# Feed-forward over the even rows of tiles first, in one program with the long convolution

## The reference, cut to what matters

```python
x = x + tanh(g_xattn[0]) * xattn(layernorm(x), ctx, mask, mask, Wq, bq, Wk, bk, Wv, bv)
x = x + tanh(g_ffn[0])   * ffn(layernorm(x), w_gate, w_up, w_down)      # quantised rows, sigmoid(gate) * up
x = x + tanh(g_xattn[1]) * longconv(layernorm(x), k, fside, ctx, ctx, 8)
x = x + tanh(g_ffn[1])   * fp8_layer(layernorm(x), w_fc, w_proj)

def longconv(v, k, bias, x1, x2, num_heads):           # B, D, L = v.shape; H = D // num_heads
    kv = vr[:, :, :, None, :] * x2r[:, :, None, :, :]  # products within a group of 8 channels
    y = causal_convolution(kv, k)                      # along L, one filter per group (by FFT in the reference)
    y = y + kv * bias
    return einsum('bhijl,bhil->bhjl', y, x1r)

def ffn(x, w_gate, w_up, w_down):
    h = sigmoid(bitlinear(x, w_gate)) * bitlinear(x, w_up)
    return bitlinear(h, w_down)                        # bitlinear: each row is scaled by its maximum and rounded
```

## Time and profile before

| | us |
|---|---|
| median of 3 runs | 1246.86 (1246.72 to 1247.12) |
| the profiled execution | 1245.74 |
| its span | 1243.9 |
| TensorE busy | 1075.5 (86%) |
| VectorE busy | 997.0 (80%) |
| ScalarE busy | 695.9 (56%) |
| GpSimd busy | 514.3 (41%) |

### The profile page before, as it was taken

One profiled execution on the slowest core, in us unless ns is written; L12 is line 12 of the kernel. 1 busy time (PEld: TensorE's weight loads), 2 busy tenths in 40 slices (PEclk: granted clock), 3 DMA queues, 4 the chain that ended last, 5 costly groups with the idle time before them and its releaser, 6 DMA issues. The chain is left out here.

```text
span 1243.9 us, 14018 instructions
## 1 busy us (share of the span) xinstructions
PE 1075.5 (86%) x4802; PEld 421.4 (34%) x4802; DVE 997.0 (80%) x1521; ACT 695.9 (56%) x835; POOL 514.3 (41%) x403
## 2 busy tenths in 40 slices
PE   4889689999999999778999967999999996279586
PEld 2444222222222222134444433444444443134232
DVE  4368679999999996298999955888788878677897
ACT  2777488888888888746666641110000000786996
POOL 2665323553543543611011017878887881000111
PEclk9999899999999999999999988999999997599889
DMA  9899733644644642051111110112212120000011
GB/s 325 268 380 385 241 114 104 194 128 136 192 125 135 197 123 92 28 195 51 35 52 35 52 38 29 57 52 68 68 51 68 52 67 1 0 1 1 18 51 68
DMA packets 73703, 132.89 MB, mean 107 GB/s; under 512 B 18336, under 2 KB 37152, under 8 KB 73120
## 3 DMA queue, kind: packets, MB, share of 16 engines
q1 hardware_dynamic: 73632, 132.00, 32.5%
HBM read 107.58 MB, written 22.02 MB: 104 GB/s over the span
## 5 line engine op out<-in xcount | busy, mean ns | idle before, releaser
L897 DVE TENSOR_REDUCE mneg<-ps_m 128x1 f32<-128x512 f32 x512 | 326.4, 685 | 40.0 <-PE ps_m L809 36.3
L1470 PE MATMUL ps_y<-kv,toeplitz_sb 128*128 128x512 f32 x640 | 279.1, 595 | 8.8 <-POOL kv L1382 8.8
L749 ACT ACTIVATE probs<-ps_s 128x1024 f32<-128x1024 f32 x256 | 250.7, 1022 | 37.9 <-PE ps_s L842 37.8
L1470 PEld LDWEIGHTS ps_y<-kv,toeplitz_sb 128*128 128x128 f32 x640 | 120.9, 191 | 154.8 <-issue 154.8
L842 PE MATMUL ps_s<-qk_stack 128*128 128x512 bf16 x512 | 139.6, 387 | 29.2 <-ACT probs L749 28.2
L852 PE MATMUL ps_o<-probs,v_all 128*17 128x512 f32 x1024 | 135.8, 603 | 0.0
L1382 POOL TENSOR_TENSOR kv<-vT,ctxT_sb 128x2048 f32<-128x2048 f32 x32 | 118.7, 3711 | 39.2 <-PE ps_y L1470 32.1
L1088 PE MATMUL ps_g<-w,xT_f 128*128 128x512 bf16 x512 | 119.6, 382 | 11.5 <-DVE h_f L1254 7.9
L809 PE MATMUL ps_m<-qk_stack 64*128 64x512 bf16 x512 | 112.1, 392 | 15.2 <-DVE mneg L897 8.1
L1435 ACT ACTIVATE w_anchor<-w_f 128x512 f32<-128x512 f32 x32 | 20.1, 628 | 180.6 <-DMA w_f<-in_w 180.6
L1536 DVE TENSOR_TENSOR z<-ps_y,ctxT_sb 128x1024 f32<-128x1024 f32 x64 | 77.9, 1218 | 46.8 <-PE ps_y L1470 46.8
(11 more groups left out here) (163 smaller groups left out, 1613.7 us busy)
## 6 DMA issues: line engine op xcount, KB each, us to landing
qk_stack<-qk_parts SPq DMA_DIRECT2D x192, 128.0 KB, 2.9
w_sweep<-in_w SPq DMA_DIRECT2D x8, 1536.0 KB, 11.8
qk_parts<-qk_part SPq DMA_DIRECT2D x16, 768.0 KB, 9.0
w_sweep<-in_w SPq DMA_DIRECT2D x16, 768.0 KB, 5.5
w_sweep<-in_w SPq DMA_DIRECT2D x16, 512.0 KB, 3.6
toeplitz_sb<-in_toeplitz SPq DMA_DIRECT2D x32, 256.0 KB, 2.6
w_f<-in_w SPq DMA_DIRECT2D x32, 256.0 KB, 2.9
v_rows<-vp SPq DMA_DIRECT2D x8, 544.0 KB, 10.0
```

Of the source, the lines that this page charges most:

```text
L749: nc.scalar.activation(pr[:, k % 2, 2 * slot:2 * slot + 2, :], S[:, 2 * slot:2 * slot + 2, :], ACT.Exp).then_inc(exp_done, 1)
L897: nc.vector.tensor_reduce(mneg[:, h, tc, hd:hd + 1], M[:, bank_, :], AX.X, ALU.max, negate=True).then_inc(max_red, 1)
L1470: mm = nc.tensor.matmul(Y[:, q % 3, l2, :], T[:, g % 2, (lt - m) * P:(lt - m + 1) * P], kv[:, g % 2, m, :], start=(m == 0), stop=(m == lt))
```

## The change

The feed-forward takes the tiles in the order 0, 2, ..., 14, 1, 3, ..., 15 (`ORDER`). `ln_vector` is cut in two: `ln_variance` issues the seven small operations up to the variance, `ln_inverse` waits for ScalarE's square root and takes the reciprocal. There are six rounds of mean and deviation instead of five: the round before the convolution is split into the even tiles (round 3, in the feed-forward's tiles 9 and 10) and the odd ones (round 4, in the convolution's groups 0 and 1). ScalarE normalises the even tiles ahead, two in each of the tiles 12 to 15, into the part of vT that the odd tiles fill later. The eight turn-ins of even tiles and their copies go between the last operations of the feed-forward; the eight of the odd tiles go beside groups 2 to 9 instead of 0 to 7.

The two stages share one block, so the engines no longer meet between them. The buffers of the convolution lie at fixed places over buffers of the feed-forward that are out of use by then, with waits for that (`xq_ready`, `hq_ready`, `h_ready`, `d_taken`). GpSimd runs the all-reduce and the first products before the last update of the feed-forward, which stands behind the gains of group 0.

The diff, cut to its core; the body of `phase_longconv` that is the same but for its indentation is left out:

```diff
+LN_COLUMNS = (range(ROWT), range(ROWT - 2), range(ROWT - 2, ROWT), range(0, ROWT, CT), range(1, ROWT, CT), range(ROWT))
+ORDER = (*range(0, ROWT, CT), *range(1, ROWT, CT))
...
-def ln_vector(core, dve, r):
+def ln_variance(core, dve, r):
...
+def ln_inverse(core, dve, r):
...
@@ tensor of phase_bitlinear
             if last:
+                pe.wait_ge(h_ready, NCH * ROWT - 1)
+                for i in range(2):
+                    turn_in(pe, i)
                 down(t - 1, 1 - par, False)
+                for i in range(2, ROWT // 2):
+                    turn_in(pe, i)
                 turn_h(t, par, False)
                 down(t, par, False)
@@ scalar of phase_bitlinear
                     copy_h(t - 1, 1 - par)
+                if c == 3 and t == ROWT // 2 + 1:
+                    ln_scalar(core, act, 3)
+                if c in (1, 3) and t >= ROWT - 4:
+                    normalise(act, 2 * (t - ROWT + 4) + c // 2)
             if last:
+                for i in range(2):
+                    place(act, i)
                 take_down(t - 1, 1 - par, False)
+                for i in range(2, 4):
+                    place(act, i)
                 round_h(t, par)
+                for i in range(4, ROWT // 2):
+                    place(act, i)
                 copy_h(t, par)
                 take_down(t, par, False)
@@ vector of phase_bitlinear
+                if c == 2 and t == ROWT // 2 + 2:
+                    ln_inverse(core, dve, 3)
+                    nc.vector.scalar_tensor_tensor(core.x_shift[:, 0:ROWT:CT], core.mean[:, 0:ROWT:CT], -1.0,
+                                                   core.rstd[:, 0:ROWT:CT], ALU.mult, ALU.mult)\
+                        .then_inc(shift_ready, 1)
...
+                if c == 3 and t == ROWT // 2 + 1:
+                    ln_variance(core, dve, 3)
             chunk_max(t, par, NCH - 1)
             if last:
                 quantise(t, par, t)
                 sweep(t, par)
-                statistics(t - 1)
-                statistics(t)
+                statistics(dve, t - 1)
@@ gpsimd of phase_bitlinear
+        for t in range(ROWT - 1):
+            update(pool, t)
@@ phase_longconv
+    def sync(sp):
+        sp.wait_ge(xf_updated, 1)
+        sp.dma_start(biasr[:], A["fside"].unsqueeze(0).to_broadcast([P, C])).then_inc(bias_loaded, 16)
+        for g in range(NGRP):
+            par = g % 2
+            if g == 0:
+                sp.wait_ge(xq_ready, ROWT)
             ...
+            sp.dma_start(T[:, par], A["toeplitz"][g]).then_inc(T_loaded[par], 16)
+            if g == 0:
+                sp.wait_ge(hq_ready, ROWT)
             ...
+            sp.dma_start(w8f[:, par], A["w8"][g]).then_inc(w8f_loaded[par], 16)
+    def rows(b):
+        return vT[:, :, b, P:2 * P]
+    def normalise_ahead(act, b):
+        if b == 0:
+            act.wait_ge(shift_ready, 1)
+        t = CT * b
+        nc.scalar.activation(rows(b), X[:, t, :].rearrange("p (l c) -> p l c", l=LT), ACT.Identity,
+                             bias=core.x_shift[:, t:t + 1], scale=core.rstd[:, t:t + 1]).then_inc(xe_ready, 1)
+    def turn_in(pe, i):
+        if i < HALF:
+            pe.wait_ge(xe_ready, i + 1)
+        else:
+            pe.wait_ge(xl_ready, i - HALF + 1)
+        if i >= 2:
+            pe.wait_ge(vT_ready, i - 1)
...
+    def gpsimd(pool):
+        pool.wait_ge(w8_run, ROWT)
+        nc.gpsimd.partition_all_reduce(w8s[:, MA, :], core.w8_max, P, bass.bass_isa.ReduceOp.max)\
+            .then_inc(w8_all, 1)
         ...
             if g % (NGRP // 2) == 0:
                 pool.wait_ge(vT_ready, ROWT if g else HALF)
+            if g == 0:
+                pool.wait_ge(h_ready, NCH * ROWT)
         ...
         for g in range(NGRP):
             products(g)
             gains(g)
+            if g == 0:
+                ffn_update(pool, ROWT - 1)
             if g:
                 skips(g - 1)
                 weights(g - 1)
@@ its scalar queue, behind the absolute values of group g
+            if g == 0:
+                ln_scalar(core, act, 4)
+            if 2 <= g < HALF + 2:
+                place(act, HALF + g - 2)
@@ its tensor queue
+            if g == 1:
+                pe.wait_ge(d_taken, ROWT)
             convolve(g, 0)
             convolve(g, 1)
+            if 2 <= g < HALF + 2:
+                turn_in(pe, HALF + g - 2)
@@ its vector queue
+            if 2 <= g < HALF + 2:
+                normalise(HALF + g - 2)
             ...
             gather(g)
+            if g == 0:
+                ffn_statistics(dve, ROWT - 1)
+                ln_variance(core, dve, 4)
+            if g == 1:
+                ln_inverse(core, dve, 4)
```

More of the change, by code:

```diff
@@ L101, in row_stats, with ln_columns @@
     core.nc.vector.bn_stats(core.bn[:, bass.ds(t, 1), :], core.X[:, bass.ds(t, 1), :]).then_inc(core.stats_step, 1)
-LN_COLUMNS = ((0, ROWT), (0, ROWT - 2), (ROWT - 2, ROWT), (0, ROWT), (0, ROWT))
-def ln_vector(core, dve, r):
-    lo, hi = LN_COLUMNS[r]
-    nc, st, tmp = core.nc, core.bn[:, lo:hi], core.ln_tmp[:, :, lo:hi]
-    n = [sum(h - l + 7 for l, h in LN_COLUMNS[0:r]) + hi - lo]
+LN_COLUMNS = (range(ROWT), range(ROWT - 2), range(ROWT - 2, ROWT), range(0, ROWT, CT), range(1, ROWT, CT), range(ROWT))
+ORDER = (*range(0, ROWT, CT), *range(1, ROWT, CT))
+def ln_columns(r):
+    cols = LN_COLUMNS[r]
+    return slice(cols.start, cols.stop, cols.step), sum(len(c) + 7 for c in LN_COLUMNS[0:r]) + len(cols)
+def ln_variance(core, dve, r):
+    cols, steps = ln_columns(r)
+    nc, st, tmp = core.nc, core.bn[:, cols], core.ln_tmp[:, :, cols]
+    n = [steps]
     dve.wait_ge(core.stats_step, n[0])
@@ L123, in ln_vector @@
     step(nc.vector.tensor_tensor(tmp[:, 0, :], st[:, :, 1], st[:, :, 4], ALU.add))
-    step(nc.vector.tensor_scalar(core.mean[:, lo:hi], tmp[:, 0, :], 0.5, None, ALU.mult))
+    step(nc.vector.tensor_scalar(core.mean[:, cols], tmp[:, 0, :], 0.5, None, ALU.mult))
     step(nc.vector.tensor_tensor(tmp[:, 1, :], st[:, :, 1], st[:, :, 4], ALU.subtract))
@@ L1022, in phase_bitlinear @@
         "ht_done", "hT_ready", "down_done", "xf_updated", "scales_ready"))
-    xf_start, hmax_ready, d_taken = sem("xf_start"), sem("hmax_ready"), sem("d_taken")
+    xf_start, hmax_ready, d_taken, shift_ready = (sem(n) for n in ("xf_start", "hmax_ready", "d_taken", "xl_shift"))
     w8c_loaded = [sem(f"w8c_loaded{i}") for i in range(2)]
@@ L1044, in sync, with tensor @@
             tile(t, t % 2, False, t == ROWT - 1)
-    def tensor(pe):
+    def tensor(pe, turn_in):
         def turn_x(t, par):
@@ L1102, in tensor, with scalar @@
         over_tiles(pe, ROWT, tile)
-    def scalar(act):
+    def scalar(act, normalise, place):
         def copy_x(t, par, first):
@@ L1158, in scalar, with statistics @@
         over_tiles(act, ROWT, tile)
+    def statistics(dve, t):
+        dve.wait_ge(xf_updated, t + 1)
+        dve.wait_ge(xf_start, 1)
+        row_stats(core, ORDER[t])
     def vector(dve):
@@ L1171, in step @@
                 dve.wait_ge(x_step, 6 * n + steps[0])
-            step(nc.vector.tensor_scalar(xn[:, par:par + 1, :], X[:, t:t + 1, :],
-                                         core.mean[:, t:t + 1], core.rstd[:, t:t + 1],
+            r = ORDER[t]
+            step(nc.vector.tensor_scalar(xn[:, par:par + 1, :], X[:, r:r + 1, :],
+                                         core.mean[:, r:r + 1], core.rstd[:, r:r + 1],
                                          ALU.subtract, ALU.mult))
@@ L1274, in tile @@
                 sweep(t, par)
-                statistics(t - 1)
-                statistics(t)
+                statistics(dve, t - 1)
         over_tiles(dve, ROWT, tile)
-    def gpsimd(pool):
[L1281 to L1289, removed]
@@ L1948, in build @@
          vector_first) = first
-        bt = phase_bitlinear(core, ctx, A, *tail)
+        bt, rest = phase_bitlinear(core, ctx, A, *tail)
+        cv, turn_in, normalise_ahead, place = phase_longconv(core, ctx, A, rest)
         with nc.Block() as block:
@@ L1956, in _ @@
                 bt.sync(sp)
+                cv.sync(sp)
             @block.gpsimd
@@ L1962, in _ @@
                 bt.gpsimd(pool)
+                cv.gpsimd(pool)
             @block.scalar
@@ L1967, in _ @@
                 at.scalar(act)
-                bt.scalar(act)
+                bt.scalar(act, normalise_ahead, place)
+                cv.scalar(act)
             @block.tensor
@@ L1974, in _ @@
                 at.tensor(pe)
-                bt.tensor(pe)
+                bt.tensor(pe, turn_in)
+                cv.tensor(pe)
             @block.vector
```

447 lines of the change are left out of this document (209 added, 238 removed).

## The result

| | median, us | runs | ratio to the kernel before, 95% |
|---|---|---|---|
| before | 1246.79 | 4 (1246.40 to 1247.12) | |
| changed | 1235.78 | 4 (1234.54 to 1236.75) | 0.9915 (0.9899 to 0.9931) |

The change makes the kernel 11.0 us faster; 1238.7 had been predicted, 8.2 less than the median then shown. The profiled execution took 1236.09 us (span 1234.3), 9.65 less than that of before.

A forecast was written before the change was run, and what follows sets the result against it. VectorE's queue bounds the feed-forward, TensorE the convolution, and GpSimd ends the gap between. Taking 10.4 us off GpSimd's path less 2.2 of delays gives 8.2 off 1246.86, so 1238.7 us; 8-in-10 range 1234.5 to 1242.5.

The forecast's parts named there:

- the likeliest case: The forecast that the earlier GpSimd path shortens the gap between stages: 1236 to 1242 us, chance 0.79.
- the sum: Net gain at the seam: 10.4 us off GpSimd's path less 2.2 of delays, 8.2 us; bounds 4.9 to 10.6.
- The reduce ahead of the last update: GpSimd's queue at the seam: the configuration runs when update(14) ends, 727.02 instead of 737.43, removing 10.4 us.
- cover: Eight turns and copies before kv go beside GpSimd's path, hiding 7 us or more; without it TensorE starts at 739.
- Update(14) later by 2.13 us: Feed-forward: small VectorE operations at tiles 9 and 10 cost 1.93 us, two turns before down(14) 0.2.
- The two turns ahead of down(14): turn_in(0) and turn_in(1) on TensorE late in the feed-forward: 0.2 us taken, bounds 0 and 0.9.
- the way into the reduce: GpSimd, from configuration to all-reduce: a change of code taken as 7.03 us, as before.
- 4. and 6.: Seam: vT ready by 733.1, down(15) ending about 739 to 740.4. Convolution start: cost 0, bounds 0 and 1.4 us.
- ScalarE's work ahead: Normalising eight even tiles in tiles 12 to 15, 0.80 us each, fits idle time: cost 0, bounds 0 and 6.4.
- Rival B: ScalarE's added work comes on the feed-forward's path: 1243.2 us, or 1246.4 with all of it; chance 0.10.
- Rival A: GpSimd's code change is not on the path; TensorE's tail sets the start at 739: gain 16.8, 1230.1 us; chance 0.07.
- Rival C: VectorE and GpSimd lock each other out in every convolution group, 1.6 us a group: 1264 us; chance 0.04.

The follow-up runs named there:

- the first repetition: The changed kernel, unaltered, timed and profiled again beside the kernel before: 1236.42 us, 0.9911 of the kernel before.
- the two repetitions: The changed kernel, unaltered, timed again twice against the kernel before: 1236.42 us (0.9911) and 1236.33 us (0.9916).
- the second profile of that kernel: Changed kernel with the maximum over partitions formed by TensorE and VectorE instead of GpSimd's all-reduce, timed again: 1227.64 us (first time 1226.34).
- VectorE's places: Against the kernel whose maximum TensorE and VectorE form: VectorE instead of ScalarE places turned rows 4 to 7; 1225.81 us, 0.9826 of the kernel before.

## Why the prediction was right

The direction, the mechanism and the place were right; the size was 1.9 us low by the profiles and 2.9 by the medians. The 11.0 us of the medians lie above the 10.6 that the sum had as its upper bound, and 1235.78 lies just below the 1236 to 1242 of the likeliest case; the 10.1 us of the profiles lie within. By its steps:

1. The reduce ahead of the last update: 10.4 us off GpSimd's path. Right; the configuration ran at the end of update(14). The two kernels that undo or do this alone show a condition that the prediction had only as cover: without the turns ahead the early start gains nothing, and the turns ahead without it gain nothing. Each half also lengthens the other chain: with update(15) still in front of it, the configuration runs at 739.2 instead of 737.4, since the work put ahead holds down(15); and the early reduce delays update(15) by 4.0 us and the last placed row by 3.3.

2. Update(14) later by 2.13 us: it came 2.13 us later (729.15 against 727.02), of which 0.34 us had arisen before the feed-forward's tile 4. The variance cost 13.48 - 12.03 = 1.45 us as said, the reciprocal and the shift 0.3 instead of 0.47. The two turns ahead of down(14), for which 0.2 was taken, cost nothing: from turn_h(14) to down(14) it is 1.95 us in both kernels (719.18 to 721.13 before, 722.77 to 724.72 in the first repetition, where all records of the matmuls are there). That both sums are 2.13 is luck: 0.34 us of the execution stand against 0.34 that the items cost less, and in the two repetitions update(14) came 3.6 us later than before. VectorE's bound was shown by doubling the work.

3. The path behind: **the term that was mis-sized is the way into the reduce**, carried over from before as 7.03 us. It took 5.6, and 5.5 to 6.2 in seven more profiles; only the kernel before has 7.0. Sorted by the loads beside it, the way in took 5.5 to 5.8 us with none (four profiles), 5.5 to 6.2 with three issued 1.2 us after its start (four), and 7.0 with five issued just as it starts (one). The way back took 6.8 to 7.7 with none (seven), 7.6 with three and 8.2 with five (one each). The five-load values are the longest of either way, but they are one profile each, and the same kernel varies by 0.6 us; that loads lengthen the code change is likely, not settled, and why the way in was shorter than the 7.03 taken stays open so far. The way back was 7.03 us against 7.12 taken, kv to the first convolution 3.84 as before. So the 8.2 of the sum, 1.4 for the way in, 0.1 for the way back and 0.3 for what item 2 took too high make 10.0; the profile has 9.76 + 0.34 = 10.1, where 0.34 is what had arisen before the feed-forward's tile 4. The other 0.9 us up to the 11.0 of the medians is in the executions chosen: the profiled one of before lay 1.1 below its median, that of the changed kernel 0.3 above its own.

4. and 6. The cover held: vT was placed by 732.7 and down(15) ended at 737.4, both within 1.6 us of the forecast. In the convolution TensorE waited for nothing that is new (waits, total, times, longest; the second line is the turn back of the last tiles, 3.9 us before as well):

```profile
PE ps_y L1516 <- POOL kv L1446: 8.6, 1, 8.6
PE ps_turn L1505 <- DVE vT L1587: 3.9, 1, 3.9
```

5. ScalarE's work ahead found its room; tiles 12, 13 and 14 take 12.03, 12.02 and 12.04 us. Rival B did not occur. The second table load of tile 9 ended at 654.35, 1.2 us after the tile's last copy on VectorE (653.18), where 2.5 had been allowed.

Rival A, that the code change is not on the path, was refuted directly: without it the convolution starts 7.7 us earlier, at the tail of TensorE. Rival C stayed with group 0. The scaling's median is still 0.62 us; the clash moved to the next instruction, once, and no group was lengthened (ns min/median/max):

```profile
L1562 DVE TENSOR_SCALAR w_anchor<-w_anchor,w_s x32: 476/620/1064, 747.8 to 1025.1; 128x512 f32<-128x512 f32 x32
...
L1565 DVE SCALAR_TENSOR_TENSOR w_f<-w_f,w_s,w_anchor x32: 753/999/4078, 748.9 to 1025.6; 128x512 f32<-128x512 f32 x32
```

## What to carry to other kernels

Where an engine shows idle time with no releaser, look at its configuration instructions before its waits: here two code changes that no instruction shows, 12.3 to 14.2 us together, set the end of the gap between two stages, and a maximum over partitions made by TensorE and VectorE removed them. That brought 8.7 us (1227.6 against 1236.3) and not 12, because TensorE's own tail then sets the start. When two chains end near each other, ask of each what it does to the other: each half of this change was worth nothing by itself. A duration that is taken over from the old place of an instruction needs its neighbours looked at too, above all the transfers that run beside it.

## What the runs showed of the hardware

A copy of 128 elements in each of two partitions took 3.3 us on VectorE when it started beside GpSimd's kv, and ended with it (734.10 + 3.32 against 733.63 + 3.71). In the second profile of that kernel it took 2.57 and again ended with kv (737.35 against 737.28), and with VectorE's places it took 3.48 (737.92 against 737.85). In that last kernel the four copies of 128x512 from PSUM, which ended before kv began, took 0.7 us each. So the price of the small copy went by the end of the product beside it, not by its own size. And the order of VectorE's operations against GpSimd's kv(1) decided which of them was long: in four profiles the scaling (3.5 to 3.6 us), in the nine where the scaling had started ahead of kv(1) the next instruction, which writes w_f (4.08).

The first 60 matmuls of the convolution take 27.6 us behind 8.8 us of idle time and 25.9 behind none. In the changed kernel the granted clock is 0.61 over the first 4.3 us, the lower of its two levels (1.2 GHz) for most of them, after an idle stretch with 0.65; without the custom instruction it is 1.00 over the same length. The first two lines are of the changed kernel, the third of the one without the custom instruction (length, busy us by engine, clock, DMA):

```profile
741.00:746.00 5.00, 0.00 (x1) 0.03 (x1) 0.00 (x0) 0.00 (x0) 3.84 (x2) 0.65 0.00 0
746.00:750.30 4.30, 4.30 (x6) 1.86 (x7) 2.82 (x3) 0.00 (x0) 4.22 (x4) 0.61 0.01 4
```

```profile
736.88:741.18 4.30, 4.30 (x12) 1.91 (x11) 3.25 (x3) 2.49 (x3) 3.91 (x3) 1.00 0.00 0
```

By the Trainium skill, "TensorE: Matmul & The Clock Gate", section "Part 1: The HAM clock gate (the "warmup" mystery)", the array runs at half speed after idling; the trace agrees, with these clocks. So closing a gap of TensorE returned more than the gap: 7.7 us of start and 1.6 of clock. The second number is not fixed. From the first convolution to the first turn of an odd tile it is 25.8 us without the custom instruction and 27.5, 27.4 and 28.8 in the three profiles of the changed kernel, so the low clock cost 1.6 to 3.0 us. It was not gone from the kernel without the custom instruction either, only smaller and elsewhere: there the last eight turns before down(15), with the clock at 0.57 around them, took 1.94 us instead of 1.11.
